# The next block's tokens: normed from the raw tokens and turned by VectorE and HBM instead of by TensorE

## The reference

```python
xn = layernorm(x)
h  = rmsnorm(xn, attn_norm_w)
# linear attention, 8 heads of 128, causal, in chunks of 128 tokens with a running state S:
#   attn = tril(q k^T);  o = attn v + q S;  S = S + k^T v;  o = rmsnorm(o, out_norm_w)
x1 = xn + o @ Wo
h2 = rmsnorm(x1, mlp_norm_w)
s  = x1 + (silu(h2 @ Wgate) * (h2 @ Wup)) @ Wdown
# the second network: every input and weight is first rounded to 4 bits in groups of 16
g  = silu(fp4_linear(silu(fp4_linear(xn, w_gate)) * fp4_linear(xn, w_up), w_down))
out = x + s * g
```

## Time and profile before

| | |
|---|---|
| median of 3 runs | 1060.57 us (1059.28 to 1060.98) |
| the profiled execution | 1059.62 us |
| its span in the profile | 1057.9 us |
| TensorE busy | 1048.9 us, 99% |
| VectorE busy | 891.3 us, 84% |
| ScalarE busy | 558.4 us, 53% |
| chain that ended last | TensorE 89%, VectorE 4%, DMA 3%, ScalarE 2% |

### The profile page before, as it was taken

How to read it: one execution, slowest core, us unless ns; L and a number is a source line. 1 busy time by engine, 2 the same in 40 slices (tenths; PEclk the granted TensorE clock), 3 DMA queues, 4 the chain that set the end, 5 groups by cost and what they waited for, 6 DMA issues and landing times.

```text
span 1057.9 us, 18981 instructions
## 1 busy us (share of the span) xinstructions
PE 1048.9 (99%) x6790; PEld 959.9 (91%) x6790; DVE 891.3 (84%) x1860; ACT 558.4 (53%) x1604; POOL 47.3 (4%) x68
## 2 busy tenths in 40 slices
PE   9999999999999999999999999999999999999998
PEld 6899999989999999998999989999999999999997
DVE  6788888888887888887777898889888888888887
ACT  6765765756757657667666634343333333333332
POOL 1000000000000000000000000101011010101010
PEclk9999999999999999999999999999999999999999
DMA  6555355455463553654446522253423233323213
GB/s 219 170 166 177 115 168 161 139 158 167 140 191 127 179 179 118 186 161 148 159 132 195 163 84 81 81 159 100 129 76 120 89 117 100 121 86 100 81 59 111
DMA packets 166238, 143.10 MB, mean 135 GB/s; under 512 B 28800, under 2 KB 162944, under 8 KB 166144
## 3 DMA queue, kind: packets, MB, share of 16 engines
q1 hardware_dynamic: 165456, 141.88, 43.2%
q10 hardware_dynamic: 688, 0.00, 0.0%
HBM read 77.27 MB, written 64.57 MB: 134 GB/s over the span
## 4 chain that ended last, share of the span: by engine, by line
PE 89%; DVE 4%; DMA 3%; ACT 2%; issue 1%; SPq 1%; DVEq 0%; ACTq 0%
PE ps L263 70%; PE ps L726 5%; PE ps L772 4%; PE ps L778 4%; PE ps L756 4%; DMA r_gate<-moved 1%; DMA moved<-work 1%; PE ps L861 1%; PE ps L614 0%; DMA work<-kept_w 0%; SPq L417 0%; DVE work L1406 0%; DMA work<-in_L_attn_hidden_states 0%; ACT work L996 0%; ACT work L969 0%
## 5 line engine op out<-in xcount | busy, mean ns | idle before, releaser
L263 PE MATMUL ps<-r_k,r_gate_up 128*128 128x512 f32 x768 | 185.2, 391 | 0.0
L263 PEld LDWEIGHTS ps<-r_k,r_gate_up 128*128 128x128 f32 x768 | 141.5, 188 | 27.2 <-DVE work L1654 0.4
L263 PE MATMUL ps<-r_o,onT 128*128 128x256 f32 x768 | 106.8, 288 | 0.0
L263 PE MATMUL ps<-r_h,r_k 128*128 128x512 f32 (+1 forms) x393 | 105.2, 403 | 0.0
L263 PEld LDWEIGHTS ps<-r_q,r_v 128*128 128x128 f32 x768 | 99.7, 191 | 4.9 <-DVE r_v L1658 0.3
L263 PE MATMUL ps<-r_q,r_v 128*128 128x256 f32 x768 | 102.3, 283 | 0.0
L969 ACT ACTIVATE work<-ps 128x128 f32<-128x128 f32 x256 | 67.1, 278 | 59.4 <-PE ps L778 59.2
L263 PE MATMUL ps<-r_h,r_q 128*128 128x512 f32 x384 | 98.2, 391 | 0.0
L263 PE MATMUL ps<-r_v,r_h 128*128 128x512 f32 x384 | 97.4, 390 | 0.0
L263 PEld LDWEIGHTS ps<-r_o,onT 128*128 128x128 f32 x768 | 95.7, 190 | 0.2
L1165 ACT ACTIVATE r_v<-work 128x512 fp32r<-128x512 f32 x64 | 40.5, 633 | 99.7 <-DVE work L1654 99.6
(11 more groups left out here) (161 smaller groups left out, 2049.3 us busy)
## 6 DMA issues: line engine op xcount, KB each, us to landing
moved<-work SPq DMA_DIRECT2D x63, 512.0 KB, 2.9
r_gate<-moved SPq DMA_DIRECT2D x252, 128.0 KB, 2.5
kept_h<-work SPq DMA_DIRECT2D x31, 384.0 KB, 2.6
work<-kept_h SPq DMA_DIRECT2D x124, 96.0 KB, 2.3
work<-in_L_attn_hidden_states SPq DMA_DIRECT2D x15, 512.0 KB, 5.1
kept<-work SPq DMA_DIRECT2D x9, 514.0 KB, 4.3
kept_h<-work SPq DMA_DIRECT2D x9, 512.0 KB, 3.5
kept_xq<-work SPq DMA_DIRECT2D x8, 512.0 KB, 5.4
```

Source lines behind the costliest of these rows:

```text
L263: done = pe.matmul(out_ap, a, b, start=first and n == 0, stop=last and n == 2, skip_group_check=skip)
```

## The change

- `turn_h` goes. The next block's tokens are normed by ScalarE straight from the raw `x_in`, with a scale and a bias for each token (`h_factors`, two small VectorE operations in step 1), at the end of step 1 and not of step 2.
- At the end of step 2's late extras VectorE turns them in 32x32 blocks from `h_flat` into `x_in` (two operations of 128x512). In step 3's exchange SyncE stores them to `kept_h` between the store to `moved` and its four loads, and loads them back to `h_flat` with four more loads behind these.
- High and low halves (`turned_hi`, `turned_lo`) move from step 3 to step 4, and read `h_flat` and not PSUM; the low halves are eight operations of 128 columns and not two of 512, and stand behind the state sums.
- The maximum for the tokens' groups moves from before the state sums of step 4 to behind those of step 3. The piece's turn moves from before the state sums of step 4 to behind the low halves.
- TensorE's `values` of step 4, and its wait for `hT_ready`, move from before the state matmuls to behind the output projection; ScalarE's copy of it moves behind its share of o's norm.
- The last block (7) prepares no next tokens and is as before, apart from the maximum's condition, which gives it the same place as before.

```diff
@@ -395 @@
-                def exchange(value, o=None, turned_o=None, again=True):
+                def exchange(value, o=None, turned_o=None, again=True, next_h=None):
@@ -408 @@
                       .then_inc(moved_out, 16)
+                    if next_h is not None:
+                        sp.wait_ge(h_turned, KD + next_h)
+                        sp.dma_start(kept_h[next_h % HALVES].rearrange("a p x -> p a x"),
+                                     in_quads(x_in.rearrange("p c d -> p (c d)"))).then_inc(h_stored, 16)
                     if again:
@@ -416 @@
                                      moved[q].rearrange("(a p) x -> p a x", a=QUADS)).then_inc(moved_in, 16)
+                    if next_h is not None:
+                        sp.wait_ge(h_stored, 16 * next_h)
+                        load_turned(h_flat, kept_h[next_h % HALVES], h_loaded)
@@ -423 @@
                         exchange(t0 + j + 2, t0 + j if not first or j else None,
-                                 t0 + j - 1 if not first or j >= LAG else None)
+                                 t0 + j - 1 if not first or j >= LAG else None,
+                                 next_h=n + 1 if h == CH - 1 and n + 1 < BLOCKS else None)
                     if first and j < HALVES:
@@ -608 @@
             def _(pe):
-                def turn_h(k):
-
-                    for c in range(CH):
-                        done = pe.transpose(ps[:, H_BANKS[k], c * P:(c + 1) * P], h_sb[:, c, k * P:(k + 1) * P],
-                                            ident[:, :])
-                    done.then_inc(h_turned, 1)
-
@@ -720 @@
                         done.then_inc(k_turned, 1)
-                    if h == CH and ahead:
-                        pe.wait_ge(hT_ready, (n0 + s) * KD + 2 * KD)
                     for c in range(CH):
@@ -740 @@
                     pe.wait_ge(v_ready, min(CH, STEPS - j) + t0 + j if final else t0 + j + CH)
-                    if ahead or h < CH:
+                    if (ahead or h < CH) and h != CH:
                         values(*((1, h, s) if h < CH else (0, h - CH, 1 - s)))
@@ -756 @@
                     done.then_inc(ds_done, 1)
-                    if h == CH - 1 and ahead:
-                        pe.wait_ge(h_ready, n0 + s + 1)
-                        pe.wait_ge(k_perm_ready, t0 + j + 2)
-                        pe.wait_ge(k_ready, t0 + j + 2)
-                        turn_h(0)
-                        pe.wait_ge(attn_ready, t0 + j + 1)
-                        turn_h(1)
-
@@ -784 @@
                         out_projection((j - LAG) % H, t0 + j - 1)
+                    if h == CH and ahead:
+                        pe.wait_ge(hT_ready, (n0 + s) * KD + 2 * KD)
+                        values(0, 0, 1 - s)
                     if final and j > PLAIN:
@@ -919 @@
-                def normed_h(parity, value):
-
-                    act.wait_ge(xn_ready, value)
-                    act.wait_ge(gu_ready, value)
+                def normed_h(n):
+
+                    act.wait_ge(h_factor_ready, n)
+                    act.wait_ge(gu_ready, n + 1)
                     for c in range(CH):
-                        done = act.activation(h_sb[:, c, :], xn[:, parity, c, :], ACT.Copy, scale=small[:, HR, c:c + 1])
+                        done = act.activation(h_sb[:, c, :], x_in[:, c, :], ACT.Identity, bias=small[:, HB, c:c + 1],
+                                              scale=small[:, HG, c:c + 1])
                     done.then_inc(h_ready, 1)
-                def turned_hi(k, parity, value, banks=H_BANKS):
-                    act.wait_ge(h_turned, value)
-                    act.activation(hT[:, parity, HI, k, :], ps[:, banks[k], :], ACT.Copy,
+                def first_turned_hi(k):
+                    act.wait_ge(h_turned, k + 1)
+                    act.activation(hT[:, 0, HI, k, :], ps[:, FIRST_H_BANKS[k], :], ACT.Copy,
                                    scale=nw_attn[:, k:k + 1]).then_inc(hT_hi, 1)
+
+                def turned_hi(parity, n):
+                    act.wait_ge(h_loaded, 16 * QUADS * n)
+                    for k in range(KD):
+                        act.activation(as_tokens(hT[:, parity, HI, k, :]), landed(h_flat, k), ACT.Copy,
+                                       scale=nw_attn[:, k:k + 1]).then_inc(hT_hi, 1)
@@ -1005 @@
                     if value <= BLOCKS:
-                        act.wait_ge(xn_ready, min(value + 1, BLOCKS))
+                        act.wait_ge(h_stored, 16 * min(value, BLOCKS - 1))
                         if value == BLOCKS:
@@ -1114 @@
                         x2_root(n0 + s + 1)
-                    if h == CH - 1 and ahead:
-                        turned_hi(0, 1 - s, (n0 + s) * KD + KD + 1)
-                        turned_hi(1, 1 - s, (n0 + s) * KD + KD + 2)
+                    if h == CH and ahead:
+                        turned_hi(1 - s, n0 + s + 1)
                     if h == CH and n0 + s in (1, 2):
@@ -1137 @@
                         o_norm_share(t0 + j + 1)
+                    if h == CH and ahead:
+                        copy_v(t0 + j + CH + 1, 0, 0)
                     if h == 0 and ahead:
                         ln_sqrt(n0 + s + 2)
-                    if h == 2 and ahead:
-                        normed_h(1 - s, n0 + s + 2)
+                    if h == 1 and ahead:
+                        normed_h(n0 + s + 1)
                 for j in range(ROLL):
@@ -1288 @@
+                def h_factors(parity, mine):
+
+                    settled(dve.tensor_tensor(small[:, HG, :], small[:, HR, :], ln_factor[:, parity, 0, :], ALU.mult), mine)
+                    dve.scalar_tensor_tensor(small[:, HB, :], mv[:, parity, :, 0], -1.0, small[:, HG, :],
+                                             ALU.mult, ALU.mult).then_inc(h_factor_ready, 1)
+
@@ -1295 @@
-                def turned_lo(k, parity, value, banks=H_BANKS):
-                    dve.wait_ge(hT_hi, value)
-                    dve.scalar_tensor_tensor(hT[:, parity, LO, k, :], ps[:, banks[k], :], nw_attn[:, k:k + 1],
-                                             hT[:, parity, HI, k, :].bitcast(F32), ALU.mult, ALU.subtract)\
+                def first_turned_lo(k):
+                    dve.wait_ge(hT_hi, k + 1)
+                    dve.scalar_tensor_tensor(hT[:, 0, LO, k, :], ps[:, FIRST_H_BANKS[k], :], nw_attn[:, k:k + 1],
+                                             hT[:, 0, HI, k, :].bitcast(F32), ALU.mult, ALU.subtract)\
                        .then_inc(hT_ready, 1)
+
+                def turned_lo(parity, n):
+                    for k in range(KD):
+                        dve.wait_ge(hT_hi, n * KD + k + 1)
+                        for c in range(CH):
+                            done = dve.scalar_tensor_tensor(as_tokens(hT[:, parity, LO, k, :])[:, c],
+                                                            landed(h_flat, k)[:, c], nw_attn[:, k:k + 1],
+                                                            as_tokens(hT[:, parity, HI, k, :])[:, c].bitcast(F32),
+                                                            ALU.mult, ALU.subtract)
+                        done.then_inc(hT_ready, 1)
@@ -1419 @@
                         fp4_add(piece, grid_w, mine, ALU.subtract)
-                    if h == CH and rounds_piece:
-                        dve.transpose(h_flat[:, 0:PIECE4[n - 1]].rearrange("p (b t) -> p b t", t=QUAD),
-                                      piece.rearrange("p (b t) -> p b t", t=QUAD)).then_inc(piece_ready, 1)
-                    if h == (0 if final else CH):
+                    if h == 0 and final:
                         fp4_max(x_of_block, x_scale, mine)
@@ -1457 @@
                         ln_stats(1 - s, n + 1, mine)
+                    if h == CH - 1 and not final:
+                        fp4_max(x_of_block, x_scale, mine)
+                    if h == CH and ahead:
+                        turned_lo(1 - s, n + 1)
+                    if h == CH and rounds_piece:
+                        dve.wait_ge(hT_ready, (n + 2) * KD)
+                        dve.transpose(h_flat[:, 0:PIECE4[n - 1]].rearrange("p (b t) -> p b t", t=QUAD),
+                                      piece.rearrange("p (b t) -> p b t", t=QUAD)).then_inc(piece_ready, 1)
                     if h == (0 if final else CH):
@@ -1469 @@
                         normalize(1 - s)
-                    if h == CH - 1 and ahead:
-                        turned_lo(0, 1 - s, n * KD + KD + 1)
-                        turned_lo(1, 1 - s, n * KD + KD + 2)
+                        dve.wait_ge(xn_ready, n + 2)
+                        dve.wait_ge(h_ready, n + 1)
+                        turn_blocks(x_in.rearrange("p c d -> p (c d)"), h_flat, h_turned)
                     if h == CH - 1 and rounds_piece:
@@ -1537 @@
                         rms_factor(1 - s, mine)
+                        h_factors(1 - s, mine)
                     if h == 3:
```

(19 more changed lines are left out.)

## The result

| | median us | lowest to highest | runs | profiled | its span |
|---|---|---|---|---|---|
| before | 1060.29 | 1059.28 to 1060.98 | 4 | 1059.62 | 1057.9 |
| after | 1076.06 | 1074.44 to 1079.2 | 4 | 1076.6 | 1074.8 |

After / before is 1.0149, 95% interval [1.0135, 1.0163]: slower by 15.8 us, where 9.6 were forecast. 1076.06 lies in the range (1059 to 1080), and 1 us above the forecast's own (1064 to 1075).

What follows compares the result with a forecast made beforehand. The prediction took a ring of engines feeding each other, late at the state sums, as the bound. Terms +2.4 + 1.25 - 2.0 + 1.7 + 6.25 = +9.6 us gave 1069.2 profiled, 1070.2 median; range 1059 to 1080.

Steps and rivals of the forecast that it cites:

- filler: Step 3's transposes, 6.1 us of step length in all, stood between the state matmuls and what needs the sums.
- rival (c): Exchange transfers collide, so the fifth step's turn of k starts at +4: 0.9 more per block, 1076; chance 0.12.
- The limits: Latest start of the state sums, after a step's first score matmul, without delay: +6.49 us even blocks, +6.2 odd.
- Step 1: Two more small VectorE operations ahead of the turn of k: +2.4 us over the blocks.
- Step 2: ScalarE's norm of the next tokens, 1.60 us, moved a step ahead: +1.25, all in block 0.
- Step 3: Transposes gone, but sums late: lengths 9.14 (odd) and 9.61 (even) against 9.78; -2.0 us in sum.
- Step 4: The fifth step: value matmuls wait for eight low-half parts, taken as 1.9 us: +1.7 in sum.
- share for late landings: In step 4, an allowance included in its 0.3 (odd) and 0.5 (even) us a block.
- Step 5: Lateness carried on: 0.5 us each in blocks 3 to 6, +2.7 in block 1, +1.55 in 2; sum +6.25.
- The factor's +12.6: In blocks 1 and 2 VectorE's factor starts at +12.6 from step 4's start, +3.3 in Step 5.
- (a): The ring has room and the removed work is won: 1054.7 us; needs a VectorE list under 9.8; chance 0.18.
- (b): Gain and loss cancel: +0.6, 1061.2 us; chance 0.10.

Runs made afterwards that it cites:

- e4: The kernel before without TensorE's 56 transposes, the turn left out of the computation: 1060.08 us, 0.9985.
- e3: The kernel after without the store and four loads of the turned next tokens through HBM: 1076.36 us, 1.0136 of before.
- e5: The kernel before with only the two added small VectorE operations of step 1, results unused: 1062.12 us, 1.0012.
- e7: The kernel after with the next tokens normed by scale alone, without the bias (Copy, not Identity): 1073.82 us, 1.0123 of before.
- e6: The kernel after with the low halves as two plain 512-column subtractions, not eight 128-column operations: 1070.72 us, 1.0088 of before.
- e9: The kernel after with e1, e2, the norms' factors behind the turns as in e8, and the next tokens' norm ahead of the share: 1064.15 us, 1.0029 of before.
- e1: The kernel after with ScalarE's value copy of step 4 moved ahead of its share of o's norm: 1073.27 us, 1.0108 of before.
- e2: The kernel after with ScalarE's rounding of the piece in blocks 1 and 2 behind the share and value copy: 1070.95 us, 1.0088 of before.
- e10: e9 with the norm's weight multiplied once into Wq, Wk and Wv, so the low halves are two plain subtractions: 1060.0 us, 0.9987 of before.
- e8: The kernel before with the norms' factors (steps 1 and 3) behind the turns of k and o, step 3's maximum behind the sums: 1061.05 us, 1.0.
- e11: e10 without the store and four loads of the turned next tokens through HBM: 1057.86 us, 0.9965 of before.

## Why the prediction was right, and where its sizes were off

The direction and the mechanism held: each step is set by what stands in front of the state sums, and by what waits for it behind them. The removed work was a filler in part: by e4 step 3 loses the full 0.87 us in odd blocks, 0.35 in even ones, nothing in block 0. The sizes were too small together. Of the 7.95 us by which the attention part went beyond the sum of +9.6, step 2 has 2.09, step 4 2.03, step 5 1.10, block 7 1.58, the rest 1.15. 1076.06 is also the number of rival (c), whose mechanism e3 rules out.

- **The limits** (+6.49 even, measured; +6.2 odd, an estimate) hold: in after, blocks 1 and 3 start step 2's sums at +6.33 and +6.32 and last 9.07, 0.16 over 8.91: a limit of +6.16; in step 3 of block 3 sums at +6.49 and 9.25 us give +6.15.
- **Step 1**: two operations cost 0.26, shown alone by e5 (I took 0.3 and 0.36). That makes +1.84 and not +2.4; that the sum came to +2.62 is luck, by the one landing in block 5.
- **Step 2, mis-sized**: the forecast took the norm's 1.60 from the kernel before, where each activation had one operand per token (the scale). The new one has two (scale and bias) and takes 596 ns instead of 503 (four: 2.07 instead of 1.70). e7 gives 1.95 of the 2.09 back (0.16 in odd blocks, about 0.36 in even ones and in block 0). By the Trainium skill (ScalarE: Activation LUTs, What ACT_TABLE_LOAD costs) each per-partition pointer operand adds about 93 ns; the two groups differ by just that. I had not applied the rule, and a term that changes an operation's operands has to be priced anew. In block 0 the delay was 1.59 where I took 1.25 (1.22 without the bias, by e7): the sums are at +8.52, and were at +6.92. Timeline of after, block 0, step 2:

```profile
35.17 1.06 PE L728 MATMUL ps<-work 128*128 128x128 f32 x8
...
38.89 2.07 ACT L924 ACTIVATE work<-work 128x256 f32<-128x256 f32 x4
...
43.69 0.94 DVE L1586 TENSOR_TENSOR work<-ps,work 128x128 f32<-128x128 f32 x3 [0.52 <-ACT work L995]
```

- **Step 3** right: 9.25 (odd) and 9.54 (even) for 9.14 and 9.61.
- **Step 4, mis-sized**: I took the middle, 1.9, between 1.4 and 2.33 for the eight parts; it was 2.18. One lasts 344 ns in this form, not the 291 that I had from the plain add, and they follow each other every 0.26 ((2.18 - 0.34) / 7). By the Trainium skill (VectorE: DVE Perf Modes, on the TRN2 errata) many small tiles pay a fixed cost each; the 2.33 by its formula was nearer than my middle. The two whole ones of e6 took 1.28, so the form costs 0.90 us a block between the sums and the values; e6 took 3.64 off step 4 with it. In before, two whole ones with the multiplication took 1.40 (from PSUM), so by estimate 0.78 of the 0.90 is the cutting into parts and 0.12 the multiplication. The 0.28 that I took too little comes to 1.96 in seven blocks, nearly the 2.03 missed. But the fit is partly luck. My share for late landings was 1.28 in all (0.3 and 0.5 a block, less the 0.06 and 0.36 by which the halves were to be late), and only block 3 had one (0.30). In exchange each block lost 0.12 to 0.14 more than its wait for the low halves (0.34 in block 1, where the step is 0.46 longer; 0.68 in block 2, 0.82 longer), since the six value products last 1.66 us behind the wait and 1.53 without one; that is 0.9 in all, and I had nothing for it. That k is in time up to +3.0 was wrong too: block 3 paid for +2.48, and in e9 a turn at +2.96 (block 4) gave a step of 10.30.
- **Step 5** right in blocks 1 (+2.56 for +2.7) and 3 to 6 (about +0.5 each for +0.5: 0.35 of waiting in block 3 and again 0.13 for the slower products); e1 and e2 show the cause. The factor's +12.6 is 12.45 by the terms written out; it was +13.0 in block 2, behind a step 4 that was also longer, so +3.3 came out by two errors that cancel. In block 2 the forecast took +1.55 and it was +2.77, with the granted clock at its low level for about 3 us (last section).
- **Block 7**, not in the sum: its code is the same, and its step 5 lasts 9.37 instead of 7.54 with the turn of k at +4.02, its step 4 7.54 instead of 8.20. VectorE waits there for landings (1.63 us in step 5), and the forecast had no term for them in this block.
- **Rivals.** (a) needs a VectorE list under 9.8 us in the fifth step; e9 and e10 show how far one gets by freeing the ring: to 1064 and 1060, not to 1054.7. (b) and (c) are out, (c) by e3 although its number fits. The price of the removed filler was right in the steps and too high in the time: e4 won 3.68 in the steps and 1.1 in the median.

Where the prediction counts eight transfers a block for the trip, the change has five (one store, four loads); no term rests on it.

**What stays open.** Why a given landing of `moved` is late. Late ones stand in other places from kernel to kernel, also in block 7, whose code the change leaves alone. That stores issued shortly before lengthen the way fits the thirteen traces of block 7 above, but no run changes that distance alone. Nor does any run take the clock's part in step 5 of block 2 out by itself.

## What to carry to other kernels

In a ring of engines (each waits for what another makes), work that is taken from the busiest engine is worth only what the next late point leaves: find for each step the start that decides it, and price what is put in front of that. Work moved behind that point isn't free either: what reads it (here six matmuls, and a rounding three stages further) becomes the next late point, so follow its readers into the next step. When a moved operation changes its operands or is cut into parts, take its price for the new form, and hold a matching total for nothing until the mechanism is shown.

## What the runs showed of the hardware that was not expected

**The clock fell behind a wait of 1.9 us.** Windows of the kernel after, block 2 step 5 (stretch, busy us and instructions of PE, PEld, DVE, ACT, POOL, then the granted clock, DMA share, GB/s):

```profile
216.00:221.00 5.00, 3.86 (x21) 2.96 (x20) 3.08 (x9) 3.79 (x17) 0.00 (x0) 1.00 0.16 64
221.00:226.00 5.00, 4.25 (x18) 3.87 (x19) 4.08 (x8) 3.55 (x8) 0.00 (x0) 0.68 0.32 108
226.00:229.00 3.00, 3.00 (x27) 3.00 (x27) 2.10 (x5) 1.44 (x10) 0.00 (x0) 0.96 0.45 131
```

TensorE waited 1.88 us for the value copy and started again at 221.75; about a microsecond later the granted clock fell to its low level, 0.50. Behind the wait the six value matmuls took 2.06 us, the eight state matmuls 1.91 and the attention product 1.51; in block 1 the first took 1.66 and the last 1.06. A mean of 0.68 between 1.2 and 2.4 GHz (0.5 and 1) is the low level for 0.64 of the 5 us. Block 1 has the same wait (1.87 us) and its clock stays at 1.00, so such a wait does not always do it:

```profile
144.46:149.46 5.00, 4.19 (x27) 3.68 (x27) 4.90 (x11) 3.11 (x7) 0.00 (x0) 1.00 0.30 105
```

The pair repeats. In e3, e6 and e7 TensorE waits 1.87, 1.75 and 1.87 us in block 2 step 5 and the clock falls to 0.50 behind it, while block 1 (1.87, 1.41, 1.87 us) keeps 1.00. In e1, where block 2 has waits of 0.23, 0.34 and 0.59 us in its place, and in e2, it keeps 1.00. What sets block 2 apart from block 1 is not shown. Step 5 is 12.71 us long in block 2 of after and 11.66 in block 1.

**The exchange through HBM has little room left.** VectorE's wait for `moved` is 7.1 us (13 times) in before and 6.3 to 9.3 (9 to 13 times) in after, e1, e2, e3, e5, e6 and e7. It is 16.2 (24) in e8, 18.8 (25) in e9, 15.5 (17) in e10 and 12.7 (15) in e11, where the factors stand behind the turns: with less work ahead of the turn the landing comes last more often. It is 11.7 (17) in e4, where TensorE has less to do. That the gains of e4 and e8 went there is read from one profile of each.
